# A graph kernel's loop rebuilt as two woven parts, with four graphs in flight

## The reference, cut to what matters

```
x += relu([n(x), M] @ W + b)         # n: normalisation; M: maximum over a node's first 25 neighbours
x += sum over 2 best of 8: w_e * (gelu(n(x) @ W1[e] + b1[e]) @ W2[e] + b2[e])    # hidden width 512
x += softmax(mask(q k^T / 4)) v @ Wo + bo     # 8 heads of 16, the mask is the adjacency
x += sum over 2 best of 6: w_e * (relu(relu(n(x) @ w1[e]) @ w2[e]) @ w3[e] + ...)   # width 128
```

## Time and profile before

| | us |
|---|---|
| median of 3 runs | 3431.71 |
| lowest, highest | 3428.62, 3441.75 |
| profiled execution, span | 3440.9 |
| TensorE, VectorE busy | 2589.0, 1840.7 |
| ScalarE, GpSimd busy | 1292.2, 837.9 |

### The profile page before, as it was taken

One profiled execution on the slowest core, in us unless ns is written; L12 is line 12 of the kernel. 1 busy time (PEld: TensorE's weight loads), 2 busy tenths in 40 slices (PEclk: granted clock), 3 DMA queues, 4 the chain that ended last, 5 costly groups with the idle time before them and its releaser, 6 DMA issues.

```text
span 3440.9 us, 48188 instructions
## 1 busy us (share of the span) xinstructions
PE 2589.0 (75%) x16137; PEld 1525.4 (44%) x16137; DVE 1840.7 (53%) x5404; ACT 1292.2 (38%) x1959; POOL 837.9 (24%) x917
## 2 busy tenths in 40 slices
PE   0018626997699878996799779995799789986697
PEld 0015423654365445554465445643465346543044
DVE  3224335843686357744685358734694379124903
ACT  1004212354334643264335433372335432452054
POOL 3533530433041502242042402252043400000000
PEclk9988867998899988998899889997899899997598
DMA  5523524422532433332542343242442241004100
GB/s 132 59 27 65 50 38 88 75 38 32 105 64 37 46 58 89 45 52 24 105 75 33 37 77 79 39 53 22 104 75 37 33 82 36 2 1 74 37 2 7
DMA packets 106030, 183.66 MB, mean 53 GB/s; under 512 B 19935, under 2 KB 56188, under 8 KB 105724
## 3 DMA queue, kind: packets, MB, share of 16 engines
q0 software_dynamic: 25344, 51.96, 17.5%
q1 hardware_dynamic: 80380, 128.07, 15.2%
HBM read 158.59 MB, written 20.97 MB: 52 GB/s over the span
## 4 chain that ended last, share of the span: by engine, by line
DVE 35%; PE 30%; issue 18%; DMA 7%; DVEq 5%; ACT 3%; SPq 1%; ACTq 0%
DVE parts L1034 15%; PE PH L1293 5%; PE PA L1339 5%; PE PY L1354 4%; PE PA L1342 4%; PE PY L1304 4%; DMA parts_dram<-parts 4%; DMA xn<-in_x 2%; DVE res_n L940 2%; ACT HB L1165 2%; DVE G L823 2%; DVEq L744 2%; DVE score L791 2%; DVE top L795 1%; DVE xn L773 1%
## 5 line engine op out<-in xcount | busy, mean ns | idle before, releaser
L716 POOL DMA_INDIRECT G<-table,slot_idx x792 | 811.4, 1024 | 372.8 <-issue 372.8
L1158 ACT ACTIVATE HB<-PH,bias_T 128x512 f32<-128x512 f32 x512 | 351.3, 687 | 862.4 <-PE PH L1293 862.4
L1034 DVE CUSTOM_DVE_ANT_0 parts<-PA,mask 128x1024 bf16<-128x1024 f32 x512 | 627.0, 1225 | 19.8 <-issue 19.8
L1165 ACT ACTIVATE HB<-PA 128x1024 f32<-128x1024 f32 x512 | 496.0, 1020 | 364.8 <-PE PA L1342 364.6
L1304 PEld LDWEIGHTS PY<-W_sb,HB 128*128 128x128 f32 x4096 | 512.3, 195 | 134.4 <-issue 87.9
L1304 PE MATMUL PY<-W_sb,HB 128*128 128x128 f32 x4096 | 521.3, 279 | 65.2 <-DVE res_n L940 53.7
L1293 PE MATMUL PH<-XT,W_sb 128*128 128x512 f32 x1024 | 527.0, 630 | 17.4 <-ACT HB L1158 17.4
L1316 PE MATMUL PA<-KS,QS 96*128 96x512 bf16 x1024 | 342.1, 420 | 114.2 <-DVE MX L1034 58.7
L1339 PE MATMUL PA<-QS,KS 99*128 99x512 bf16 x1024 | 393.6, 384 | 11.2 <-ACT HB L1165 7.4
L1342 PE MATMUL PA<-identb,mask 128*128 128x128 bf16 x4096 | 397.1, 218 | 0.0
L594 POOL TENSOR_TENSOR pool_pad<-pool_pad 1x1 f32<-1x1 f32 x112 | 23.6, 210 | 1520.4 <-DVE slot_idx L803 1275.0
(11 more groups left out here) (156 smaller groups left out, 2270.1 us busy)
## 6 DMA issues: line engine op xcount, KB each, us to landing
adj_sb<-in_adj SPq DMA_DIRECT2D x64, 512.0 KB, 4.2
adjm<-in_adj SPq DMA_DIRECT2D x64, 512.0 KB
G<-table,slot_idx POOLq DMA_INDIRECT x792
parts_dram<-parts SPq DMA_DIRECT2D x16, 768.0 KB, 6.9
QS<-parts_dram SPq DMA_DIRECT2D x48, 256.0 KB, 8.3
KS<-parts_dram SPq DMA_DIRECT2D x48, 256.0 KB, 8.1
xn<-in_x SPq DMA_DIRECT2D x8, 512.0 KB, 13.1
table<-xn SPq DMA_DIRECT2D x8, 512.0 KB, 3.5
```

What stands on the lines that cost most here:

```text
L716: pool.indirect_dma_start(G[:, t % 2, s, :], None, table, bass.IndirectOffsetOnAxis(slot_idx[:, t, s:s + 1], axis=0), bounds_check=ROWS - ...
L1034: ins = dve.tensor_tensor_reduce(out=junk, in0=psum(ps, step)[:, :], in1=mask[:, t, :], scale=1.0, scalar=LOWEST, op0=ALU.add, op1=ALU.max ...
L1158: act.activation(HB[:, i % 2, c, :], psum(ps, step)[:, :], ACT.Gelu, bias=bias_T[:, e * HC + c:e * HC + c + 1]).then_inc(*emptied(ps, step))
L1165: act.activation(HB[:, kc % 2, 2 * pr:2 * pr + 2, :], psum(ps, key)[:, :].rearrange("p (h q) -> p h q", h=2), ACT.Exp, scale=float(D) ** - ...
```

## The change

The passes stay, with the same instruction kinds and the same products. What a pass holds is cut anew: its `att` part starts with the value products of graph b; the scores are those of graph b+1; the dense mixture is that of graph b+2, right behind its first layer; finds, fetches and maxima are those of graph b+3, the graph loaded in the same pass. A plan with threads (lists in order), gates (what must have been placed) and a table of durations replaces `weave` and `spread`: at each step it takes the thread whose next step could begin first. The adjacency has one buffer instead of two, the residual of the sparse part and the deviations get tensors of their own, scratch that lay in `mask` and `HB` moves to `parts` and XT2, small chain steps are cut in single engine shares, router banks move from the PA ring to PH, and queries and keys are loaded by head halves (`stack`).

```diff
+COURSE = {
+    "take": [("DVE", 1.6)], "shift": [("DVE", 0.7)], "load_res": [("SP", 6.0)], "lnv": [("DVE", 2.8)],
...
+    "mask": [("DVE", 0.95)], "s": [("PE", 0.44), ("DVE", 1.42)], "mparts": [("DVE", 2.6)], "mT": [("PE", 0.4)],
...
+EXPERTS = ("up0", "down0", "u1", "u2", "y1")
+LEAD = {"u1": 10.0, "u2": 10.0, "y1": 10.0}
+EAGER = {"acc0": 3.0, "acc1": 3.0, "find": 2.0, "pmax": 2.0, "s": 1.2}
+def course(step):
+    k = step[0]
+    if k == "find":
+        return [("DVE", 9.0 if step[1] == 0 else 4.5)]
+    if k == "gather":
+        return [("POOL", 36.0 if step[1] == 0 else 23.0 if step[1] < 3 else 12.5)]
...
+def planned(att, unit, near, load):
...
+    if load:
+        p.chain([("load_x",), ("lnv", 0), ("sq", 0), ("ln", 0), ("store_x",)])
+        p.gate(("load_x",), ("gT",) if near else None)
+        p.threads.append([("pmax", t) for t in range(TILES)])
+        p.threads.append([("gather", t) for t in range(TILES)])
+        p.chain([k for t in range(TILES) for k in (("load_adj", t), ("deg", t), ("class", t), ("find", t))])
+        p.gate(("find", 0), ("shift",))
+        for t in range(TILES):
+            p.gate(("gather", t), ("find", t), ("store_x",), ("pmax", t - 2) if t >= 2 else None)
+            p.gate(("pmax", t), ("gather", t))
+        if not near:
+            p.threads.append([("load_w",)])
+            p.gate(("load_w",), ("load_adj", 0))
...
+        p.chain([("stack", 0), ("stack", 1)])
+        p.gate(("stack", 0), ("sp", 1), ("st", 1, 0, TILES - 1) if att else None)
+        p.gate(("stack", 1), ("st", 1, 1, TILES - 1) if att else None)
...
+        p.gate(("s", 0, 0), ("stack", 0), ("gnn_add",) if near else None)
+        p.gate(("s", 0, GH), ("stack", 1))
...
+        p.gate(("up0", 0, 0), ("lg0",), last_av)
+        p.gate(("down0", 0, 0), ("ba", 0))
...
 def schedule(att, unit, near, load):
...
+    while any(h < len(t) for h, t in zip(heads, p.threads)):
+        best = None
+        for n, (h, t) in enumerate(zip(heads, p.threads)):
+            if h == len(t) or not all(g in ended for g in p.gates.get(t[h], [])):
+                continue
...
+            found = tried(t[h])
+            if found is not None:
+                rank = 20.0 + 30.0 * h / len(t) - LEAD.get(t[h][0], 0.0) if t[h][0] in EXPERTS else n
+                score = (round(found[0], 2), rank)
...
     if k in ("lg0", "lg1"):
-        return A(k)
+        return H(k)
...
                     elif kind == "load_adj":
                         t = step[1]
-                        sp.wait_ge(*at(ps, turn, "adjf", ("find", t - 2)))
-                        sp.dma_start(adj_sb[:, t % 2, :], adj_v[b + 2, t, :, :]).then_inc(S[f"adj{t % 2}"], 16)
+                        sp.wait_ge(*at(ps, turn, "adjf", ("find", t - 1) if t >= 1 else None))
+                        sp.dma_start(adj_sb[:, :], adj_v[b + 3, t, :, :]).then_inc(S["adj"], 16)
...
             def body(ps, turn, b):
-                if ps.near:
-                    pool.wait_ge(*at(ps, turn, "tab"))
+                if ps.load:
+                    pool.wait_ge(*at(ps, turn, "tab", ("store_x",)))
...
                     elif kind == "take":
-                        settle(dve.tensor_copy(res_b[:, :, :], res_n[:, :, :]).then_inc(S["took"], 1))
+                        if ps.att:
+                            dve.wait_ge(*at(ps, turn, "out"))
+                            settle(dve.tensor_copy(res_f[:, :, :], res_b[:, :, :]))
+                        if ps.unit:
+                            dve.tensor_copy(res_b[:, :, :], res_n[:, :, :])
+                        settle(dve.memset(dve_pad[:, 3:4], 0.0).then_inc(S["took"], 1))
```

More of the change, by code:

```diff
@@ L49 @@
 ORDER0 = [(hf, e) for hf in range(2) for e in range(E0)]
-FINDS_EARLY = 10
 ORDER1 = [(hf, e) for hf in range(2) for e in range(E1)]
+N0, N1 = len(ORDER0), len(ORDER1)
 CLASS_SLOTS = (8, 16)
[L55 to L97, removed]
@@ L100, in schedule @@
-def schedule(att, unit, near, load):
[L105 to L235, removed]
-    if load:
-        chain += [("load_x",)]
-    if near:
-        chain += [("cha", 0), ("chb", 0), ("chc", 0)]
-    if load:
-        chain += [("lnv", 0), ("ln", 0), ("store_x",), ("next_adj", 0), ("next_adj", 1)]
-    experts1 = []
-    if att:
-        n1 = len(ORDER1)
-        for k in range(n1 + 3):
-            if k < n1:
-                experts1.append(("u1", k))
-            if 1 <= k <= n1:
-                experts1.append(("u2", k - 1))
-            if 2 <= k <= n1 + 1:
-                experts1.append(("y1", k - 2))
-            if k >= 3:
-                experts1.append(("acc1", k - 3))
-    s += spread(experts1, chain) if experts1 else chain
-    if att:
-        assert s.index(("chb", 1)) < s.index(("acc1", 0))
-        s.append(("store",))
-    if load and not near:
-        s.append(("load_w",))
@@ L273, in signals @@
     if k == "gT":
-        return sum([H("xn", hf) + A("agg", hf) for hf in range(2)], [])
+        return sum([H("xn", hf) + H("agg", hf) for hf in range(2)], [])
     if k == "gnn":
-        return Y("gnn", 0) + Y("gnn", 1)
+        return H("gnn", 0) + H("gnn", 1)
     if k == "gnn_add":
@@ L588, in graph_kernel, with settled @@
         block = ctx.enter_context(nc.Block())
+        def settled(eng, place):
+            name, value = place
+            return name, value if isinstance(value, int) else eng.snap(value)
         def held_by(eng, pad, pool=False):
@@ L922, in add_biases @@
                 dve.drain()
+            def add_biases(ps, turn, step):
+                layer = step[1]
                 res = (res_n, res_f)[layer]
@@ L996, in body @@
                         gnn_add(ps, turn)
+                    elif kind == "sm":
+                        level(ps, turn)
                     elif kind == "cha":
@@ L1000, in body @@
                         weigh(ps, turn, step)
-                    elif kind == "chc":
+                    elif kind == "wc":
+                        weights_out(ps, turn, step)
+                    elif kind == "ba":
                         add_biases(ps, turn, step)
@@ L1064, in body @@
                         dve.drain()
+                    elif kind == "finc":
+                        _, qh, g = step
                         key = ("ctx", qh, g)
@@ L1167, in body @@
                                                    ACT.Exp, scale=float(D) ** -0.5).then_inc(*emptied(ps, key))
-                    elif kind == "proj":
-                        copy_out(XB[:, half[step[1]]], ps, turn, ("ctxT", step[1]))
+                    elif kind == "projt":
+                        copy_out(ctxT, ps, turn, ("ctxT", step[1]))
                     elif kind == "t1":
@@ L1182, in body @@
                         act.wait_ge(*is_full(ps, turn, step))
[L1183 to L1184 removed]
+                        if (kind, j) == ("u1", 0) and ps.unit:
+                            act.wait_ge(*at(ps, turn, "pd", ("sp", 1)))
+                        k, col = (j % 2, EB1) if kind == "u1" else (2, EB2)
+                        act.activation(HE[:, k, :], psum(ps, step)[:, :], ACT.Relu,
                                                bias=bias_T[:, col + e:col + e + 1]).then_inc(*emptied(ps, step))
```

435 lines of the change are left out of this document (311 added, 124 removed), and 4 rows, old and new, of the table COURSE.

## The result

| | before | changed |
|---|---|---|
| median, us | 3434.57 (4 runs) | 3349.82 (4 runs) |
| lowest, highest | 3428.62, 3441.75 | 3342.10, 3350.98 |
| profiled execution, span | 3440.9 | 3349.0 |

The ratio is 0.975, with a 95% interval of 0.9723 to 0.9777: 85 us less, where I forecast 19 less. The direction and the range held; the size didn't.

A forecast was written before the change was run, and what follows sets the result against it. No engine bounds throughout: TensorE idles 57 us a turn, and GpSimd's serial fetches are a hidden second limit. Fill 751, five turns of 384, 12 for graph 6 and end 739 give 3422 us, 3413 for the median; range 3320 to 3520.

The forecast's parts named there:

- head, with the branch: Start of a turn to first slot indices: 3.7 us of branch plus 57 us of VectorE's list, waits and first find.
- fill: Passes before the steady loop, with finds and fetches started early: 751 us, a gain of 204 over before.
- passes 5, 6, 7: The last three passes, behind the loop, with value products, chains, experts and remaining scores: 739 us against 980.
- step 4: Scores, experts, accumulations behind last neighbour maximum: VectorE's 120 us and TensorE's 121 overlap with loss, 137 us, bounds 121 and 157.
- 121 x 1.13: TensorE's 121 us behind the last neighbour maximum, times a loss factor from the old scores-beside-mixture stretch: 137 us.
- rival B: Tail of a turn: VectorE and TensorE wait for each other, factor 1.30, 157 us, total 3522, median 3513; chance 0.17.
- -241, +204 and +19: Whole kernel, change in us: the end loses 241, the fill gains 204, the loop gains 19.
- rival D: Ahead of the first indices: ScalarE's table switches cost 8 us more a turn, total 3462, median 3453; chance 0.05.
- Step 3: First indices to last neighbour maximum: serial fetches take 186 us, 198 for graph 6, leaving TensorE 77 us idle.
- Rival A: Loop: fetches hide and TensorE bounds, a turn of 331 us, total 3145, median 3136; chance 0.10.
- rival C: Fetches slow beside denser VectorE work: up to 74 us a turn, total 3792, median 3783; chance 0.05.
- The traces' signs: In the loop: fetch waits over 500 us, last maximum about 243 us into a turn, a turn of 376 to 396.

The follow-up runs named there:

- experiments 1 and 6: Changed kernel with extra work: 1, up products doubled ahead of last maximum 3351.9 us, behind 3401.0; 6, eight VectorE operations in tail, lump 3430.9, spread 3401.5.
- experiment 4: Changed kernel with the loop's steps behind the last neighbour maximum merged evenly, as the kernel before did, instead of by planner times: 3385.1 us.
- Experiment 5: Kernel before, with finds 0 and 1 moved from the scores into the value products: 3857.1 us (one run).
- experiment 3: Both kernels with every tile fetching only 8 slots, 64 fetches a turn instead of 97: changed kernel 3073.9 us, kernel before 3259.8 us.
- the best version: Changed kernel with measured fetch and find times plus further planner numbers, such as a longer expert lead and TensorE times by 1.03: 3102.8 us, ratio 0.9046.
- the measured costs: Changed kernel with only the planner's fetch and find times raised to those of the trace: 3129.9 us, ratio 0.912 to the kernel before.

## Why the prediction was right, and where it was wrong

**The frame held.** A turn is a head to the first indices, a serial chain of fetches, and what the order left behind the last maximum. Each part was predicted apart (means of five turns, head with its branch, tail without):

| | predicted | measured | five turns |
|---|---|---|---|
| head, with the branch | 60.7 | 58.0 | -13 |
| indices to last maximum | 186, graph 6 12 more | 191.2 | +14 |
| tail | 137 | 126.3 | -54 |
| fill | 751 | 746 | -5 |
| passes 5, 6, 7 | 739 | 725 | -14 |

The sum is -72, and 3422 - 3349 = 73. The head's -13 and the chain's +14 cancel.

**The step that failed is step 4, the term "121 x 1.13".** 121 us of TensorE's steps took 126.3, a factor of 1.04. I took 1.13 from the stretch of scores beside the mixture before, argued that two lists of equal length can't overlap without loss, and so held it for a fair value or even too low (rival B, 1.30). Measured: both lists are nearly full (experiments 1 and 6), and they overlap with 5 us of loss in 126. Where the 1.13 came from, the runs show in part: the even merge. Put back, it costs the tail 5.9 us of the missing 10.7, and the turn 7.2 (experiment 4). The windows tell what kind of loss that is. In 939:1089 TensorE was idle for 8.4 us, and busy for 141.6 with steps that I had sized at 132.5, a factor of 1.07. The even tail has about the same idle time, 8.1 us, but is busy for 124.3 with my 121, a factor of 1.03, as in the changed kernel. So the idle part of the 1.13 belongs to the even merge; why the same kinds of step kept TensorE busy for longer beside the finds and fetches of the kernel before is open. Experiment 5 took the finds out there, and the stretch lost 3.6 us. The same factor, used once more in pass 5, gave 322 instead of the measured 305; with five turns that is 71 of the 73 us.

Why this made the forecast, -19, four times too small: it was a difference of -241, +204 and +19, and an error of 11 us in 384 counts five times.

**Head.** The list and its waits came out 3 us shorter. The input load, 12.95 us in the chain before, is no longer waited for: it is issued at 1122.12, behind the transposes, and the norm that needs it comes 11 us later, without a wait. No wait for a store stands between the mark and the first indices either, where I had put 3.9 us.

**ScalarE's switches (rival D).** 15 table loads lie in the turn 1121 to 1495, and in the head VectorE waits 1.7 us in all for the square roots, where I had put 3.5. ScalarE's timeline around a square root:

```profile
1121.88 1.94 ACT L1246 ACTIVATE HB<-PA 128x1024 f32<-128x1024 f32 x2
1123.84 1.28 ACT L1200 ACT_TABLE_LOAD   x1
1125.13 0.21 ACT L1200 ACTIVATE sq<-sd 128x8 f32<-128x8 f32 x1
```

A switch is 1.28 us here, with 20 ns ahead of it and 10 behind; VectorE waited 1.38 us for this root. The Trainium skill (ScalarE: Activation LUTs, What ACT_TABLE_LOAD costs) adds a drain of 1380 ns to the load; this trace doesn't show one, and the measurement decides.

**Step 3 and the rivals.** The chain of 186 us was 187 to 189 in four turns and 203.6 for graph 6, where I had put 198. Step 3 called the 77 us between TensorE's 166 us of steps and the last maximum idle. The first two windows show 51 us of idle time, as TensorE was busy for 191 us with these steps, at a granted clock of 0.85 in the middle; the time is the same, since the fetches set it. Rival A (fetches hide, a turn of 331) is wrong for this kernel: experiment 3 takes fetches away and gains 27.7 us a turn. But its turn exists: the best version has 334, with order alone. Rival B is refuted by the tail; rival C, as a large term, by the fetches' median, 997 ns as before. In small it is there: 68 of the 792 fetches took over 1.2 us, where 40 did, and all of them together lie 44 us over 997 ns each, where it was 22. The traces' signs came as announced: waits over 500 us, the last maximum at 242 us; only the turn, 375.5, fell just under the 376 to 396 given.

**Fill and end.** The last three passes took 305, 243 and 178 us (322, 247, 170 predicted). In the pass before the loop two errors cancelled: the indices came 24 us earlier than I said, but the fetches wait for the table behind both splits, and so took 208 from there, not 186.

## What to carry to other kernels

Where one serial chain of an idle-looking engine sets a period, read three lengths: to its start, its own, and what the order leaves behind it; then ask which of them the order can fill. A planner is only as good as its durations: fetch times raised by 35.5 us and find times by 9.5 us in a turn took 38 us from every turn, and a table read from a trace gave back 220 us with the same instructions in another order. A loss factor taken from a stretch belongs to the order in that stretch, not to the pair of engines; and an engine with a busy share of 84% can have next to no room, if the gaps between its operations are part of their price.

## What the hardware showed beside this

**The granted clock is higher where the order fills the hole.** With the same 16137 products TensorE is busy for 2576.5 us in the changed kernel and, on its page, for less with the measured costs:

```profile
PE 2521.7 (81%) x16137; PEld 1502.7 (48%) x16137; DVE 1838.2 (59%) x5404; ACT 1338.7 (43%) x1993; POOL 856.3 (27%) x917
```

The mean granted clock is 0.900 in the first and 0.924 in the second; in the middle of a turn it is 0.85, with TensorE 75% busy, and 0.94, with 87%. Of its two levels, 1.2 and 2.4 GHz, the higher is thus held for more of the stretch.

**Fetches are slower beside certain VectorE work.** 68 of the 792 fetches took more than 1.2 us. GpSimd's timeline at the start of tile 1, and VectorE's neighbour maximum at the same time:

```profile
1208.16 1.00 POOL L782 DMA_INDIRECT G<-table,slot_idx  x1 [0.30 <-issue]
...
1216.80 2.52 POOL L782 DMA_INDIRECT G<-table,slot_idx  x1 [6.50 <-issue]
```

```profile
1216.68 2.80 DVE L890 TENSOR_TENSOR G<-G 128x1536 f32<-128x1536 f32 x2 [1.14 <-issue]
```

By overlap, 67 of the 68 lie beside the finds (L858, L862) and the neighbour maxima (L890, L893), which read wide tiles from SBUF, and none beside the row maxima, one of whose inputs is in PSUM (in the kernel before 4 of some 170 there). The Trainium skill (GPSIMD Engine Reference, Specifications) tells of contention with VectorE operations that have two SBUF inputs or are in a 2-port perf mode; L858 and L890 have two inputs, but 16 long fetches lie mainly beside L862, which reads one. No run here separates them, as L862 follows L858 directly, and none shows in which mode L862 ran.
